# Down and up of a step side by side, one tile transposed by VectorE, base splits a pair earlier, no GpSimd drain

## The chip, the cores and the metric

One NeuronCore of one Trainium2 chip runs the kernel. The metric is the device time of one execution in microseconds (us); of the kernel before, three runs gave 684.30 (median), 684.29 and 685.31. A core has the engines TensorE (PE; its weight loads are listed as PEld), VectorE (DVE), ScalarE (ACT), GpSimd (POOL) and SyncE (SP), each with its own instruction stream, which meet only through semaphores.

## The reference, cut to what matters

Two layers, each an adapter chosen per sequence, then a feed-forward part, with a residual. The routed low-rank part of layer 0 is a sum over 8 experts, two of which carry weight.

```python
# x (32 sequences, 64 tokens, 1024), ids (32,)
c  = einsum('bsi,boi->bso', x, L0_cond_weight[ids])          # 16 adapters of 1024x1024
w  = normalised top-2 of softmax(c @ W_router.T)             # 8 experts
h  = einsum('td,erd->ter', c, lora_A)                        # rank 16
x1 = x + c @ W_base.T + b_base + 2 * einsum('ter,eor,te->to', h, lora_B, w)
y  = einsum('bct,bcd->bdt', x1, L1_cond_weights[ids])        # 64x64 mix over a sequence's tokens
t  = y[:, perm].reshape(-1, 16, 64)                          # 16 heads
u  = gelu(einsum('bhd,hdm->bhm', t, up))                     # hidden 256
t  = einsum('bhm,hmd->bhd', u, down)
out = x1 + t[:, argsort(perm)]
```

## The kernel before, in words

The work has two phases. In the adapter phase 16 pairs of sequences, sorted by adapter, go through the 1024x1024 adapter product in fp32 (`adapter_blocks`, 8 blocks of rows for each pair); VectorE turns the result of a pair with 32x32-block transposes (`turn_pair`, L797), TensorE computes router and low-rank products from it (`router`, L437), VectorE makes the routing weights (`route`), TensorE turns them (`turn_hw`) and GpSimd keeps the pair in `c_all`. In the last pair (number 15) the adapters' ring of buffers comes free block by block, and `base_t`, which lies in the same memory, is filled: ScalarE writes the leading part of W_base as fp32r (`base_leading(j)`, L641) and VectorE the rest (`base_rest(j)`, L868). The last pair's own result goes another way: ScalarE and VectorE copy it out (`out_of_acc`), TensorE turns it (`turn`), both copy it again.

The second phase has 4 groups of 8 sequences (512 tokens) and, in each, 8 steps of 128 output rows, 32 steps in all, written as a loop over groups with the steps of a group unrolled (`over_steps`). A step (g, j) of TensorE's queue holds work of three steps: the base product of step j in 4 parts (`base`: for each of two row blocks two fp32r matmuls with `c_hi`, L505, then one each with `c_lo`, L510) and 3 low-rank matmuls (`lora`, L518 to L520), after which VectorE adds bias and residual (`layer0_out`, L916) into one of 4 `xres` buffers; of step j-1 the 4 transposes of that tile to token rows (`to_tokens`, L403), which ScalarE copies to `x1_tok` (`x1_tokens`, L681), the mix (`mix_tokens`, L533), the split of its result into `y_hi` (ScalarE, L690) and `y_lo` (VectorE, L926) and the up product (`up_heads`, L546, 64-row tiles, two heads side by side); of step j-2 the four gelus (ScalarE, L677), the down product (`down_heads`, L555, 64-column tiles, two heads side by side) and the final add (`result`, L932), after which GpSimd stores the tile by an indirect DMA (`store`, L376), and, when that has landed, fetches the next tile into the same buffer (`refill`, L322). In the last step of a group, `c_leading` (ScalarE) and `c_rest` (VectorE, L904) split the next group's `c`.

The order of every engine's queue is written by hand. TensorE's before, in one step:

```python
base(g, j, 0)
to_tokens(j1)
base(g, j, 1)
down_heads(g2, j2)
mix_tokens(g1, j1)
base(g, j, 2)
base(g, j, 3)
lora(g, j)
up_heads(g1, j1)
```

SyncE loads `up_raw` for the next step once `up_rest` has read it, and `down_sb` (two buffers) once a down product is done, in one queue in that order. The eight PSUM banks are all in use: 0 to 3 for up, 4 for `c_ps`, 5 for `tr_ps`, 6 for the mix, 7 for down.

## Time and profile before

| what | value |
|---|---|
| profiled execution | 684.34 us, of it 682.5 us from the first to the last instruction |
| matmuls, weight loads | 3266, 3267 |
| VectorE busy | 277.4 us (41%) |
| ScalarE busy | 158.8 us (23%) |
| GpSimd busy | 128.2 us (19%) |
| DMA | 102.86 MB, mean 151 GB/s |

A timeline row gives start, duration, engine, line, operation, destination and source tiles, and how many instructions are merged in it; in brackets stands how long the engine was idle before it and what ended that. Starts of successive rows on TensorE are the better measure of cost, since matmuls overlap: one may be listed with 0.39 us while the next starts 0.23 us later.

### The profile page before, as it was taken

To read this page: it belongs to the slowest core of one execution; us is meant where nothing else is said; L and a number is where in the kernel's file an instruction comes from. 1 tells how busy PE (TensorE), PEld (TensorE's weight loads), DVE (VectorE), ACT (ScalarE), POOL (GpSimd) and SP (SyncE) were. 2 spreads that over 40 slices of the span, in tenths; PEclk is the share of its full clock that TensorE was granted. 3 is DMA by queue.
4 is the path that set the end of the run, shared out by engine and by line. 5 is a ranking of instruction groups with operands and counts; after the bars stand their busy time and mean duration, and the time that the engine had idled before them with its cause. 6 is when DMAs were issued, how large, how long until landed. Compare 5 with 4: busy or idle time off the path is not lost.

```text
span 682.5 us, 10584 instructions
## 1 busy us (share of the span) xinstructions
PE 641.7 (94%) x3266; PEld 366.1 (54%) x3267; DVE 277.4 (41%) x714; ACT 158.8 (23%) x294; POOL 128.2 (19%) x194
## 2 busy tenths in 40 slices
PE   3899999999999999887999999999999999999992
PEld 3334434434333433374767676767676666666660
DVE  2046666666656666773212421214221225121220
ACT  3100000000000000344232633234333244323241
POOL 5000001111111100300222222222222222222201
PEclk9799999999999999979999999999999999999997
DMA  8998671459595959300222222222222222222200
GB/s 292 411 405 311 241 286 36 172 184 392 191 396 182 402 174 404 106 17 9 77 67 80 63 78 61 79 65 79 61 77 63 79 65 77 62 77 63 78 31 31
DMA packets 42298, 102.86 MB, mean 151 GB/s; under 512 B 8322, under 2 KB 17538, under 8 KB 42242
## 3 DMA queue, kind: packets, MB, share of 16 engines
q1 hardware_dynamic: 34370, 80.24, 32.8%
q0 software_dynamic: 6784, 21.51, 9.4%
q10 hardware_dynamic: 1088, 0.56, 0.3%
q14 instruction: 44, 0.36, 0.2%
q8 instruction: 12, 0.20, 0.1%
HBM read 93.89 MB, written 8.39 MB: 150 GB/s over the span
## 4 chain that ended last, share of the span: by engine, by line
PE 86%; DMA 5%; DVE 2%; issue 2%; SPq 1%; ACT 1%; POOL 0%; ACTq 0%; DVEq 0%; POOLq 0%
PE wide L423 27%; PE bank L505 18%; PE bank L555 9%; PE bank L510 8%; PE wide L546 7%; DMA ring<-adapters_dram 5%; PE bank L533 5%; PE bank L437 4%; PE bank L403 3%; DVE base_t L868 1%; PE bank L518 1%; PE bank L519 1%; PE bank L520 1%; SPq L227 1%; PE bank L443 1%
## 5 line engine op out<-in xcount | busy, mean ns | idle before, releaser
L423 PE MATMUL wide<-ring,x_in 128*64 128x512 f32 x1024 | 228.3, 599 | 7.9 <-DMA ring<-adapters_dram 7.6
L423 PEld LDWEIGHTS wide<-ring,x_in 128*64 128x64 f32 x1024 | 72.8, 137 | 148.0 <-issue 142.5
L505 PE MATMUL bank<-c_hi,base_t 128*128 128x512 f32 x496 | 142.8, 409 | 0.8 <-DVE base_t L868 0.8
L797 DVE STREAM_TRANSPOSE c_pair<-wide 32x256 f32<-32x256 f32 x240 | 107.1, 446 | 63.7 <-issue 34.3
L505 PEld LDWEIGHTS bank<-c_hi,base_t 128*128 128x128 f32 x496 | 86.3, 189 | 25.0 <-issue 11.7
L677 ACT ACTIVATE act_sb<-wide 128x512 f32<-128x512 f32 x128 | 66.3, 603 | 101.7 <-PE wide L546 101.7
L932 DVE TENSOR_TENSOR xres<-bank,xres 128x512 f32<-128x512 f32 x32 | 22.1, 691 | 162.7 <-PE bank L555 162.7
L510 PE MATMUL bank<-c_lo,base_t 128*128 (+1 forms) x248 | 77.0, 391 | 0.0
L376 POOL DMA_INDIRECT out_dram<-xres,row_out x32 | 34.4, 1075 | 208.3 <-DVE xres L932 208.3
L555 PE MATMUL bank<-act_sb,down_sb 128*64 128x512 f32 x256 | 62.0, 605 | 1.5 <-issue 1.5
L637 ACT ACTIVATE small<-small 128x1 f32<-128x1 f32 x16 | 3.2, 203 | 249.1 <-DVE small L833 249.1
L354 POOL COPY c_all<-c_pair 128x512 f32 x30 | 17.5, 610 | 230.0 <-DVE c_pair L797 230.0
L510 PEld LDWEIGHTS bank<-c_lo,base_t 128*128 128x128 f32 x248 | 46.6, 188 | 10.8
L322 POOL DMA_INDIRECT xres<-xT_dram,row_in x32 | 36.1, 1130 | 77.8 <-DMA out_dram<-xres,row_out 74.5
L916 DVE SCALAR_TENSOR_TENSOR xres<-bank,bias,xres 128x512 f32<-128x512 f32 x31 | 23.3, 750 | 59.3 <-PE bank L520 59.3
L533 PEld LDWEIGHTS bank<-mix_sb,x_tok 128*128 128x128 f32 x256 | 31.0, 191 | 25.5 <-issue 24.3
L690 ACT CAST y_hi<-bank 128x512 fp32r<-128x512 f32 x32 | 18.8, 587 | 100.5 <-PE bank L533 100.5
L533 PE MATMUL bank<-mix_sb,x_tok 128*128 (+1 forms) x256 | 37.0, 287 | 0.9 <-ACT x_tok L681 0.9
L437 PE MATMUL bank<-ar_sb,c_pair 128*128 128x136 f32 x256 | 34.1, 289 | 0.8 <-DVE c_pair L806 0.8
L437 PEld LDWEIGHTS bank<-ar_sb,c_pair 128*128 128x128 f32 x256 | 33.2, 202 | 2.0 <-DVE c_pair L806 1.2
L555 PEld LDWEIGHTS bank<-act_sb,down_sb 128*64 128x64 f32 x256 | 15.7, 136 | 31.0 <-issue 30.9
L926 DVE TENSOR_TENSOR y_lo<-bank,y_hi 128x512 fp32r<-128x512 f32 x32 | 22.1, 692 | 21.5 <-ACT y_hi L690 21.1
(111 smaller groups left out, 477.0 us busy)
## 6 DMA issues: line engine op xcount, KB each, us to landing
ring<-adapters_dram SPq DMA_DIRECT2D x120, 512.0 KB, 7.1
x_in<-x_seq_dram SPq DMA_DIRECT2D x32, 256.0 KB, 7.6
up_raw<-up_dram SPq DMA_DIRECT2D x64, 64.0 KB, 2.3
down_sb<-down_dram SPq DMA_DIRECT2D x32, 128.0 KB, 2.3
ar_sb<-lora_a_router_dram ACTq DMA_DIRECT2D x1, 544.0 KB, 4.4
mix_sb<-mix_dram SPq DMA_DIRECT2D x32, 16.0 KB
xres<-xT_dram,row_in POOLq DMA_INDIRECT x32, 3.4
out_dram<-xres,row_out POOLq DMA_INDIRECT x32, 3.1
```

Of the source, the lines that this page charges most:

```text
L322: pool.indirect_dma_start(dst, None, table, bass.IndirectOffsetOnAxis(ap=rows, axis=0)) \
L376: pool.indirect_dma_start(out_rows, bass.IndirectOffsetOnAxis(ap=row_out[:, j:j + 1], axis=0), xres[:, j % XBUF, :], None).then_inc(stored ...
L423: last = pe.matmul(acc[half][h][z * TOK:(z + 1) * TOK, :], x_in[:, half, z, k, :], ring[:, k, z, h * HALF:(h + 1) * HALF], start=(k == 0), ...
L437: last = pe.matmul(router_ps[:, 0:AR], c_pair[:, k, :], ar_sb[:, k, :], start=(k == 0), stop=(k == KT - 1))
L505: pe.matmul(c_bank(g, j)[:, :], base_t[:, j, w, k, :], c_hi[:, k, :], start=(k == 0 and w == 0), stop=False)
L510: last = pe.matmul(c_bank(g, j)[:, :], base_t[:, j, 0, k, :], c_lo[:, k, bass.ds(g * GT, GT)], start=False, stop=False)
L533: last = pe.matmul(y_ps[:, p * P:(p + 1) * P], x1_tok[:, p * P:(p + 1) * P], mix_sb[:, bass.ds(g % 2, 1), p, :].rearrange("c a d -> c (a d)"),
L546: last = pe.matmul(u_ps[2 * m + head][:, :], w[rows, m * P:(m + 1) * P], y[rows, :], start=(n == 0), stop=(n == 2))
L555: last = pe.matmul(d_ps[head * HD:(head + 1) * HD, :], down_sb[:, j % 2, head, m, :], act_sb[:, 2 * m + head, :], start=(m == 0), stop=(m ...
L677: nc.scalar.activation(act_sb[:, i, :], u_ps[i][:, :], ACT.Gelu).then_inc(act_ok, 1)
L797: last = nc.vector.transpose(c_pair[r * SQ:(r + 1) * SQ, :, q * SQ:(q + 1) * SQ], wide[half][q * SQ:(q + 1) * SQ, :, :] .rearrange("p h (k ...
L916: nc.vector.scalar_tensor_tensor(out=xres[:, b, :], in0=c_bank(g, j)[:, :], scalar=bias[:, j:j + 1], in1=xres[:, b, :], op0=ALU.add, op1=A ...
```

## The change

TensorE's queue: in a step, down of step j-2 and up of step j-1 now stand together at the end, after `lora`; the mix of step j-1 stands between base parts 2 and 3; `to_tokens` is gone from all steps but 1 and the last. In its place VectorE transposes the tile by 16 block transposes from `xres` straight to `x1_tok` (`x1_turned`), so the ScalarE copy is gone there too. `down_heads` waits for each half of its gelus apart, and for the result two steps earlier. VectorE's `result` moves from step j-2 to step j-3 of its queue; `gelu` moves from j-2 to j-1 in ScalarE's, and `up_leading` is made a step earlier, behind the gelus. In the last pair, ScalarE begins the base splits before the tanh of pair 14, and VectorE makes three of them (0, 1, 4) before that pair's routing, two behind it, one (5) after the last pair's tiles, and two in step 1. `b_lo` is made before the last pair's tile is turned back; in step 1 base part 3 stands ahead of `to_tokens`, and up no longer waits for that step's tile. The block is closed without GpSimd's drain.

```diff
@@ -54,6 +54,7 @@
 BIG = -3.0e38
 SEQ_BITS = 5
 CS = KT // 2
+SPLIT_ORDER = (0, 1, 4, 2, 3, 5, 6, 7)
 GATHERS = range(PAIRS // 4, PAIRS // 4 + KT)
 
 
@@ -155,7 +156,8 @@
         base_ps = [banks[4:6], banks[2:4]]
         b_ps = banks[0:2]
         sorted_ps = banks[7]
-        u_ps, c_ps, tr_ps, y_ps, d_ps = banks[0:4], banks[4], banks[5], banks[6], banks[7]
+        u_ps, c_ps, y_ps, d_ps = banks[0:4], banks[4], banks[6], banks[7]
+        second_ps, tr_ps = banks[5], (banks[7], banks[5])
 
 
         ids_in, sort_ids_in, perm_in, ar_in, b_in, bias_in, mix_in, up_in = (
...
@@ -207,13 +209,13 @@
         def c_bank(g, j):
 
 
-            return u_ps[3] if early(g, j, 2) and j == 1 else c_ps
+            return second_ps if early(g, j, 2) and j == 1 else c_ps
 
         def early(g, j, n):
 
             return isinstance(g, int) and g * STEPS + j < n
 
-        block = ctx.enter_context(nc.Block())
+        block = ctx.enter_context(nc.Block(no_gpsimd_drain=True))
 
 
         @block.sync
...
@@ -548,9 +550,10 @@
                     last.then_inc(u_done, 1)
 
             def down_heads(g, j):
-                pe.wait_ge(act_ok, (g * STEPS + j) * 4 + 4)
                 pe.wait_ge(down_in[j % 2], (g * (STEPS // 2) + j // 2 + 1) * 16)
+                pe.wait_ge(fin_ok, g * STEPS + j)
                 for m in range(2):
+                    pe.wait_ge(act_ok, (g * STEPS + j) * 4 + 2 * m + 2)
                     for head in range(2):
                         last = pe.matmul(d_ps[head * HD:(head + 1) * HD, :], down_sb[:, j % 2, head, m, :],
                                          act_sb[:, 2 * m + head, :], start=(m == 0), stop=(m == 1),
@@ -559,22 +562,23 @@
 
             def first_step():
 
+                pe.wait_ge(base_ok, 1)
                 for part in range(CS):
                     base(0, 0, part)
-                base(0, 1, 0)
-                base(0, 1, 1)
+                pe.wait_ge(base_ok, 2)
+                for part in range(2):
+                    base(0, 1, part)
                 turn_hw(PAIRS - 1)
                 base(0, 1, 2)
                 pe.wait_ge(b_ok, 1)
                 lora(0, 0)
 
             def second_step():
+                base(0, 1, 3)
                 pe.wait_ge(x1_ok, 1)
-                to_tokens(0)
-                base(0, 1, 3)
+                to_tokens(0, 0)
                 lora(0, 1)
                 mix_tokens(0, 0)
-                pe.wait_ge(x1_ok, 2)
                 up_heads(0, 0)
                 pe.wait_ge(base_ok, KT)
 
@@ -587,24 +591,20 @@
                     return
                 g1, j1 = (g, j - 1) if j >= 1 else (g - 1, STEPS - 1)
                 g2, j2 = (g, j - 2) if j >= 2 else (g - 1, STEPS + j - 2)
-                base(g, j, 0)
-                to_tokens(j1)
-                base(g, j, 1)
+                for part in range(CS - 1):
+                    base(g, j, part)
+                mix_tokens(g1, j1)
+                base(g, j, CS - 1)
+                lora(g, j)
                 down_heads(g2, j2)
-                mix_tokens(g1, j1)
-                base(g, j, 2)
-                base(g, j, 3)
-                lora(g, j)
                 up_heads(g1, j1)
 
-            pe.wait_ge(base_ok, 6)
             over_steps(pe, step)
             pe.wait_ge(x1_ok, LAST)
-            to_tokens(STEPS - 1)
+            to_tokens(STEPS - 1, 1)
             mix_tokens(GROUPS - 1, STEPS - 1)
             down_heads(GROUPS - 1, STEPS - 2)
             up_heads(GROUPS - 1, STEPS - 1)
-            pe.wait_ge(fin_ok, LAST - 1)
             down_heads(GROUPS - 1, STEPS - 1)
 
 
@@ -646,16 +646,19 @@
                     last = nc.scalar.copy(base_rows[:, j, h * KT // 2:(h + 1) * KT // 2, :],
                                           base_ps[j % 2][h][:, :].rearrange("p (k o) -> p k o", o=P))
                 last.then_inc(base_turned, 1)
-            with act.Fori(0, PAIRS - 1) as t:
+            with act.Fori(0, PAIRS - 2) as t:
                 tanh(t)
-            for j in range(0, 6):
+            for j in range(0, 5):
                 base_leading(j)
+            tanh(PAIRS - 2)
             act.wait_ge(b_tr, 1)
-            act.wait_ge(base_ok, 5)
+            act.wait_ge(base_ok, 3)
             for h in range(2):
                 last = nc.scalar.copy(b_hi[:, h * KT // 2:(h + 1) * KT // 2, :],
                                       b_ps[h][:, :].rearrange("p (j o) -> p j o", o=P))
             last.then_inc(b_hi_ok, 1)
+            for j in range(5, 7):
+                base_leading(j)
             seqs = last_seqs(act)
             out_of_acc(PAIRS - 1, 1)
             turned(PAIRS - 1)
...
@@ -691,44 +694,37 @@
 
             def step(g, j):
                 g1, j1 = (g, j - 1) if j >= 1 else (g - 1, STEPS - 1)
-                g2, j2 = (g, j - 2) if j >= 2 else (g - 1, STEPS + j - 2)
                 if early(g, j, 1):
-                    act.wait_ge(base_ok, 6)
+                    act.wait_ge(base_ok, 5)
                     act.wait_ge(c_kept, PAIRS * 2)
                     act.wait_ge(last_kept, 4)
                     for part in range(CS):
                         c_leading(g, part)
+                    base_leading(7)
+                    up_leading(g, j)
                     tanh(PAIRS - 1)
+                    act.wait_ge(base_ok, 6)
                     act.wait_ge(hw_t_ok, PAIRS * 2)
                     hw_leading(g)
-                    base_leading(6)
-                    base_leading(7)
-                elif j == 0:
+                    return
+                if j == 0:
                     act.wait_ge(c_done, g * STEPS)
                     hw_leading(g)
                 splits = j == STEPS - 1 and not (isinstance(g, int) and g == GROUPS - 1)
-                if not early(g, j, 2):
-                    for i in range(4):
-                        gelu(g2, j2, i)
+                if early(g, j, 2):
+                    x1_tokens(0)
                 if splits:
-                    c_leading(g + 1, 0)
-                if not early(g, j, 1):
-                    x1_tokens(g1, j1)
+                    for part in range(CS - 1):
+                        c_leading(g + 1, part)
+                y_leading(g1, j1)
                 if splits:
-                    c_leading(g + 1, 1)
-                if not early(g, j, 1):
-                    up_leading(g1, j1)
-                    y_leading(g1, j1)
-                if splits:
-                    c_leading(g + 1, 2)
-                    c_leading(g + 1, 3)
+                    c_leading(g + 1, CS - 1)
+                for i in range(4):
+                    gelu(g1, j1, i)
+                up_leading(g, j)
 
             over_steps(act, step)
-            for i in range(3):
-                gelu(GROUPS - 1, STEPS - 2, i)
-            x1_tokens(GROUPS - 1, STEPS - 1)
-            gelu(GROUPS - 1, STEPS - 2, 3)
-            up_leading(GROUPS - 1, STEPS - 1)
+            x1_tokens(1)
             y_leading(GROUPS - 1, STEPS - 1)
             for i in range(4):
                 gelu(GROUPS - 1, STEPS - 1, i)
@@ -880,21 +876,24 @@
                 pair(i * 2 + 2, 0)
             pair(PAIRS - 3, 1)
             turn_pair(PAIRS - 2, 0)
+            for j in SPLIT_ORDER[0:3]:
+                base_rest(j)
             hw_turned(PAIRS - 3)
             route(PAIRS - 2)
-            for j in range(0, 6):
+            for j in SPLIT_ORDER[3:5]:
                 base_rest(j)
             seqs = last_seqs(dve)
             out_of_acc(PAIRS - 1, 1)
-            turned(PAIRS - 1)
-            keep_last(1, seqs)
-            hw_turned(PAIRS - 2)
             dve.wait_ge(b_hi_ok, 1)
             for h in range(2):
                 ks = slice(h * KT // 2, (h + 1) * KT // 2)
                 last = nc.vector.tensor_tensor(b_lo[:, ks, :], b_ps[h][:, :].rearrange("p (j o) -> p j o", o=P),
                                                b_hi[:, ks, :].bitcast(F32), ALU.subtract)
             last.then_inc(b_ok, 1)
+            turned(PAIRS - 1)
+            keep_last(1, seqs)
+            hw_turned(PAIRS - 2)
+            base_rest(SPLIT_ORDER[5])
             dve.wait_ge(bias_in, KT * 16)
 
 
@@ -931,35 +930,51 @@
                 dve.wait_ge(d_done, g * STEPS + j + 1)
                 nc.vector.tensor_tensor(xres[:, b, :], d_ps[:, :], xres[:, b, :], ALU.add).then_inc(fin_ok, 1)
 
+            def x1_turned(g, j):
+
+                b = j % XBUF
+                dve.wait_ge(x1_ok, g * STEPS + j + 1)
+                for q in range(P // SQ):
+                    for f in range(P // SQ):
+                        last = nc.vector.transpose(
+                            x1_tok[q * SQ:(q + 1) * SQ, :].rearrange("p (c f) -> p c f", f=P)[:, :, f * SQ:(f + 1) * SQ],
+                            xres[f * SQ:(f + 1) * SQ, b, :].rearrange("p (c q t) -> p c q t", c=GP, t=SQ)[:, :, q, :])
+                last.then_inc(x1_tok_ok, 1)
+
             def step(g, j):
                 g1, j1 = (g, j - 1) if j >= 1 else (g - 1, STEPS - 1)
-                g2, j2 = (g, j - 2) if j >= 2 else (g - 1, STEPS + j - 2)
+                g3, j3 = (g, j - 3) if j >= 3 else (g - 1, STEPS + j - 3)
                 if early(g, j, 1):
                     for part in range(CS):
                         c_rest(g, part)
                     route(PAIRS - 1)
                     hw_turned(PAIRS - 1)
+                    hw_rest(g)
+                    layer0_out(g, j)
+                    return
+                if not early(g, j, 3):
+                    result(g3, j3)
+                up_rest(g1, j1)
+                if early(g, j, 2):
+                    for i in SPLIT_ORDER[6:8]:
+                        base_rest(i)
                 if j == 0:
                     hw_rest(g)
                 splits = j == STEPS - 1 and not (isinstance(g, int) and g == GROUPS - 1)
                 if splits:
                     c_rest(g + 1, 0)
                     c_rest(g + 1, 1)
-                if not early(g, j, 2):
-                    result(g2, j2)
-                if not early(g, j, 1):
-                    up_rest(g1, j1)
-                    y_rest(g1, j1)
+                y_rest(g1, j1)
                 if splits:
                     c_rest(g + 1, 2)
                 layer0_out(g, j)
+                if not (isinstance(g, int) and g == GROUPS - 1 and j == STEPS - 1):
+                    x1_turned(g, j)
                 if splits:
                     c_rest(g + 1, 3)
-                if early(g, j, 2) and j == 1:
-                    base_rest(6)
-                    base_rest(7)
-
-            over_steps(dve, step)
+
+            over_steps(dve, step, 3)
+            result(GROUPS - 1, STEPS - 3)
             up_rest(GROUPS - 1, STEPS - 1)
             y_rest(GROUPS - 1, STEPS - 1)
             result(GROUPS - 1, STEPS - 2)
```

## Rows read from the trace of the kernel before

**Rows 1.** The page: busy time, share and count of TensorE; granted clock in 40 slices.
```profile
PE 641.7 (94%) x3266; PEld 366.1 (54%) x3267; DVE 277.4 (41%) x714; ACT 158.8 (23%) x294; POOL 128.2 (19%) x194
...
PEclk9799999999999999979999999999999999999997
```
**Rows 2.** Timeline of TensorE over one step of the second phase.
```profile
341.93 1.19 PE L505 MATMUL bank<-c_hi,base_t 128*128 128x512 f32 x4
342.96 0.62 PE L510 MATMUL bank<-c_lo,base_t 128*128 x2
343.42 0.60 PE L403 MATMUL bank<-ident,xres 128*128 128x128 f32 x4
343.77 1.18 PE L505 MATMUL bank<-c_hi,base_t 128*128 128x512 f32 x4
344.79 0.62 PE L510 MATMUL bank<-c_lo,base_t 128*128 x2
345.34 1.94 PE L555 MATMUL bank<-act_sb,down_sb 128*64 128x512 f32 x8
347.21 1.16 PE L533 MATMUL bank<-mix_sb,x_tok 128*128 x8
...
349.59 1.07 PE L505 MATMUL bank<-c_hi,base_t 128*128 128x512 f32 x4
350.50 0.62 PE L510 MATMUL bank<-c_lo,base_t 128*128 x2
...
351.41 0.39 PE L520 MATMUL bank<-hw_lo,b_hi 128*128 x1
351.73 0.50 PE L546 MATMUL wide<-y_hi,up_hi 64*128 64x512 f32 x2
...
353.31 1.20 PE L505 MATMUL bank<-c_hi,base_t 128*128 128x512 f32 x4
```
**Rows 3.** Timeline of TensorE: the first matmuls of step 2 and of step 31.
```profile
319.13 1.18 PE L505 MATMUL bank<-c_hi,base_t 128*128 128x512 f32 x4 [0.81 <-DVE base_t L868]
...
649.46 1.20 PE L505 MATMUL bank<-c_hi,base_t 128*128 128x512 f32 x4
```
**Rows 4.** Timeline of VectorE: the add behind that step's lora.
```profile
351.94 0.75 DVE L916 SCALAR_TENSOR_TENSOR xres<-bank,bias,xres 128x512 f32<-128x512 f32 x1 [2.22 <-PE bank L520]
```
**Rows 5.** Timeline of VectorE: the transposes of one pair in the adapter phase.
```profile
204.65 7.34 DVE L797 STREAM_TRANSPOSE c_pair<-wide 32x256 f32<-32x256 f32 x16 [1.90 <-PE wide L423]
```
**Rows 6.** Groups by shape, 340 to 680 us: busy, mean ns, idle before.
```profile
L932 DVE TENSOR_TENSOR xres<-bank,xres 128x512 f32<-128x512 f32 x30 | 20.7, 691 | 151.0 <-PE bank L555 151.0
...
L921 DVE TENSOR_TENSOR up_lo<-up_raw,up_hi 128x256 fp32r<-128x256 f32 x29 | 12.1, 416 | 3.0 <-ACT up_hi L686 3.0
```
**Rows 7.** The page's DMA issues: count, KB, median us from issue to landing.
```profile
up_raw<-up_dram SPq DMA_DIRECT2D x64, 64.0 KB, 2.3
```
**Rows 8.** Timeline of GpSimd: one fetch alone, one beside VectorE's `c_rest`.
```profile
352.74 1.06 POOL L322 DMA_INDIRECT xres<-xT_dram,row_in  x1 [2.52 <-DMA out_dram<-xres,row_out]
...
387.46 1.73 POOL L322 DMA_INDIRECT xres<-xT_dram,row_in  x1 [2.55 <-DMA out_dram<-xres,row_out]
```
**Rows 9.** Timeline of TensorE from the last pair to step 1.
```profile
292.32 1.97 PE L403 MATMUL bank<-ident,c_tok 128*128 128x128 f32 x8 [4.88 <-ACT c_tok L620]
295.08 3.76 PE L437 MATMUL bank<-ar_sb,c_pair 128*128 128x136 f32 x16 [0.78 <-DVE c_pair L806]
...
310.98 0.66 PE L403 MATMUL bank<-ident,xres 128*128 128x128 f32 x4 [0.84 <-DVE xres L916]
...
316.67 0.50 PE L546 MATMUL wide<-y_hi,up_hi 64*128 64x512 f32 x2 [2.06 <-DVE xres L916]
```
**Rows 10.** Timeline of VectorE in the last pair: the base splits.
```profile
284.48 6.89 DVE L868 TENSOR_TENSOR base_t<-base_rows,base_t 128x1024 fp32r<-128x1024 f32 x6
```
**Rows 11.** Timeline of TensorE behind the last step.
```profile
668.50 1.94 PE L555 MATMUL bank<-act_sb,down_sb 128*64 128x512 f32 x8 [1.51 <-issue]
```
**Rows 12.** Instructions of line 64, the block's end: count, min/median/max ns, starts.
```profile
L64 POOLq DRAIN  x1: 7268/7268/7268, 675.0 to 675.0; - x1
```

More of the change, by code:

```diff
@@ L189, in build, with over_steps @@
         bias_rows = b_base.rearrange("(d a) -> d a", a=1)
-        def over_steps(eng, step):
-            step(0, 0)
-            step(0, 1)
+        def over_steps(eng, step, first=2):
+            for j in range(first):
+                step(0, j)
             with eng.Fori(0, GROUPS - 1) as g:
-                for j in range(2, STEPS + 2):
+                for j in range(first, STEPS + first):
                     step(g + j // STEPS, j % STEPS)
-            for j in range(2, STEPS):
+            for j in range(first, STEPS):
                 step(GROUPS - 1, j)
@@ L521, in lora, with to_tokens @@
                           start=False, stop=True).then_inc(c_done, 1)
-            def to_tokens(j):
-                transposes([tr_ps], [xres[:, j % XBUF, p * P:(p + 1) * P] for p in range(GP)], tr_done)
+            def to_tokens(j, way):
+                transposes([tr_ps[way]], [xres[:, j % XBUF, p * P:(p + 1) * P] for p in range(GP)], tr_done)
             def mix_tokens(g, j):
@@ L677, in gelu, with x1_tokens @@
                 nc.scalar.activation(act_sb[:, i, :], u_ps[i][:, :], ACT.Gelu).then_inc(act_ok, 1)
-            def x1_tokens(g, j):
-                act.wait_ge(tr_done, g * STEPS + j + 1)
-                nc.scalar.copy(x1_tok[:, :], tr_ps[:, :]).then_inc(x1_tok_ok, 1)
+            def x1_tokens(way):
+                act.wait_ge(tr_done, way + 1)
+                nc.scalar.copy(x1_tok[:, :], tr_ps[way][:, :]).then_inc(x1_tok_ok, 1)
             def up_leading(g, j):
```

## The prediction

> **What bounds the kernel now.** I read the page's busy shares first: TensorE is busy 94% of the span, VectorE, the next, 41% [rows 1]. A busy TensorE need not be a well used one, so the timeline of one step comes next, read by the starts of successive rows [rows 2]. There is no idle bracket in it: weight loads, transposes and matmuls follow each other. From the start of step 2 to that of step 31 the distance is 649.46 - 319.13 = 330.33 us for 29 steps, 11.39 us each [rows 3]. In this phase an instruction taken off TensorE's queue is time gained, as long as what replaces it elsewhere arrives before TensorE asks for it. At the phase's beginning and end it is otherwise: there TensorE waits for VectorE and ScalarE, and at the very end for GpSimd.
>
> **The sum** is made against the profiled execution, 684.34 us, which is the median of the runs (684.30) within 0.04. I go through it in four places.
>
> **1. The steps.** The four transposes take 343.77 - 343.42 = 0.35 us. The base part behind them takes 344.79 - 343.77 = 1.02 for its four L505, where one behind other base work takes 350.50 - 349.59 = 0.91: each change of kind costs the follower 0.11. Both go: 0.46. Up begins 351.73 - 351.41 = 0.32 after the last lora matmul, against 0.91/4 = 0.23 inside a row of such matmuls: 0.09 for going from full tiles to row tiles. Before, a step enters down from base (344.79 to 345.34 is 0.55, the two L510 need 342.96 to 343.42 = 0.46, so 0.09) and up from lora (0.09); now down is entered from lora and up from down, whose 1.87 us (345.34 to 347.21) hold the way out of column tiles already. So one entry of 0.09 goes. The mix, now behind base, may lose a little of its entry too; unseen in these rows, it is between 0 and 0.06, and I take 0.02, nearer the end at which nothing happens, because no row shows the mix behind full tiles in a steady step [rows 2]. A step becomes 11.39 - 0.57 = 10.82; 29 steps give 16.5 us (bounds 0.45 and 0.62 a step: 13.0 and 18.0).
>
> The page TensorEngine Tiling (Array Packing) of the Trainium skill, section Key Properties, says that changing the tiling mode drains TensorE. By that rule alone one drain of four goes; the rows above price it at 0.09, a small part of the gain.
>
> **Does the replacement arrive in time?** Count from the start of down, D, which now follows lora. VectorE's add starts 351.94 - 351.73 = 0.2 after TensorE's next group and takes 0.75 [rows 2, 4], so transposes start at D + 1.0. No such transpose is in the trace; the nearest is 32x256, 16 of them in 7.34 us or 459 ns each [rows 5]. From 256 to 512 elements a VectorE instruction grows from 416 to 691 ns, 1.07 ns an element [rows 6], so 128 elements fewer are 137 ns less: 322 ns, 5.2 us for 16. The source is SBUF and not PSUM, which I count as no difference; the upper bound is the untouched 7.34, the lower 4.5. The tile is ready at D + 6.25. TensorE asks for it after down (1.87), up (353.31 - 351.73 = 1.58) and three base parts (1.03 + 0.46, then 0.91 + 0.46 twice: 4.23), at D + 7.68 [rows 2]. Slack 1.4 us: hidden. At the upper bound the tile comes at D + 8.4, 0.7 late.
>
> The page VectorE: DVE Perf Modes of the Trainium skill, section Rules for kernel authors, speaks against this edit: transpose 128x128 on TensorE if PSUM will do as destination. The rows agree that TensorE is far quicker at it (0.35 us and a copy against about 5.2); what they add is which engine the 0.35 us is taken from.
>
> What else moves, in each queue. VectorE: behind the transposes stand `result` (0.69) and `up_rest` (0.42) [rows 6], done at about D + 7.4; then y's rest, which needs the mix, and the next add, at D + 11. Its step holds 2.55 + 5.2 = 7.8 us of 10.8. In a group's last step four `c_rest` (as long as a base split of the same size, 1.15, below) and `hw_rest` are added; walking them in order, the third delays the add by about 0.6, the transposes end about 1.2 us before the mix, and the fourth `c_rest` is done some 2 us before base part 3 wants it. So I cost the three borders at nothing; without that cover each would be 1 to 2 us. ScalarE, busy 23% in all [rows 1], loses the copy; its gelus run right behind up, and the down that wants them comes 7 us later. The added wait of down for `result` two steps back is met 4 us early; behind it in TensorE's queue stand down and up. `result` comes some 8 us later than before, so the store and refetch by GpSimd start later, about 9 us in all, against 21 us until the buffer is wanted. SyncE: the load of `up_raw` stands in its queue behind the wait for a down that is now at the step's end; it is issued behind down (D + 1.9) and `down_sb`'s load, and lands 2.3 us after issue [rows 7], about D + 5.5. ScalarE wants it behind its gelus, at about D + 5, and VectorE's `up_rest` at D + 7: half a microsecond on ScalarE, hidden by the transposes. All cost nothing.
>
> Beside VectorE's SBUF work GpSimd's fetch instruction is stretched from 1.06 to 1.73 us [rows 8]; there is slack of 7 us for it.
>
> **2. The beginning.** Before, TensorE waits 4.88 us for the last pair's tile: VectorE makes six splits of 6.89/6 = 1.15 us from 284.48 on [rows 9, 10] and only then copies the tile. Now three come before the routing, mostly in VectorE's idle time (delaying the routing by about 0.5), and two remain behind it: 285.0 + 2.3 + 0.7 gives the tile at 288.0 where `turn` started at 292.32: 4.2 us. The granted clock has a digit 7 in the 18th slice, 290 to 307 [rows 1], where these waits lie, and the 16 router passes of 3.76 us [rows 9] are at the 1.2 GHz level; with a wait of 1 us instead of 4.88 I take them at 2.4 GHz, half as long. Not all of that 1.9 + 0.9 counts, because then base waits about 0.5 for the first `c_lo`, which VectorE now delivers behind `b_lo` and one split: 2.1 us. In steps 0 and 1 the wait of `to_tokens` for the add (0.84) is filled by base part 3; the wait before up goes from 2.06 to about 1.6; the wait for the last splits, 0.81, goes [rows 3, 9]. Sum 4.2 + 2.1 + 0.8 + 0.5 + 0.8 = 8.4 us (bounds 4.2, the first term alone, and 9.5).
>
> **3. The end.** Step 31 saves its transposes, 0.46, and the 0.09. ScalarE now has one gelu and `up_leading` before the token copy (about 1.0), for which the mix waits. The last down, which waits 1.51 for all four gelus, starts after two [rows 11]: 0.9 earlier. Sum 0.5 us gained (bounds: 1.0 lost, 1.4 gained).
>
> **4. The drain.** GpSimd's DRAIN of 7268 ns starts at 675.0, when the last store has landed, and the span ends at 682.5 [rows 12]. Nothing else happens meanwhile. Without it: 7.2 us gained. Bounds 0, if the same work is then waited for elsewhere or outside the span, and 7.3.
>
> **Forecast:** 16.5 + 8.4 + 0.5 + 7.2 = 32.6; 684.3 - 32.6 = **651.7 us**. Bounds: 13.0 + 4.2 - 1.0 + 0 = 16.2 (668.1) and 18.0 + 9.5 + 1.4 + 7.3 = 36.2 (648.1).
>
> **The rivals.**
> *The beginning gives only its first term.* The clock stays low behind the shorter wait, or base waits for `c_lo`. For it: VectorE has the same work, only shifted. 651.7 + 4.2 = 655.9.
> *The drain does not vanish.* Its time is real bookkeeping for GpSimd's DMAs, and the end may wait for it in another way. 651.7 + 7.2 = 658.9. Against it: DMA had landed and no engine worked on.
> *The transposes cost per instruction, not per element.* Then 7.34 us, 0.7 late in 29 steps: 20.6 less gain, 672.3. For it: half-sized instructions never run here. Against: 416 against 691 ns.
> *Slower: VectorE and GpSimd stretch each other.* If the 16 transposes are stretched as GpSimd's fetch is (1.73/1.06 = 1.63), they take 8.5 us, the mix waits 1.9 us in every step, 54 us in all: 706. It decides from 7.75 us for 16 on (484 ns each), where the wait of 1.1 us a step eats all 32.6. Against it: only GpSimd's side of such an overlap is seen stretched, and its own work takes a quarter of a step.
>
> **How the numbers follow.** Forecast 0.67, beginning 0.11, drain 0.10, per-instruction cost 0.07, slower 0.03, nothing gained overall 0.02. The first alone spans 648.5 to 654.5; the range that leaves out the last three kinds is 648.0 to 660.0. All cases but the last two are faster by over 0.2% (1.4 us), about what a measurement of this kernel can tell from no change: faster 0.95, same 0.01, slower 0.04.
>
> **What would show it.** Right: starts of `base` part 0 10.8 us apart in TensorE's timeline, no idle bracket before the mix; a group of 16 x 30 transposes 32x128 of about 320 ns; idle before `turn` about 1 us and router passes at full granted clock; no POOL DRAIN in the block's end, and a span ending 0.3 us after the last store lands. Wrong: an idle time of TensorE before L533 put down to VectorE, step 2 starting later than 313, transposes above 410 ns, a DRAIN or a longer time outside the span.

## The result and the profile after

The changed kernel takes 651.83 us (median; 650.76 to 653.02), the kernel before, measured beside it, 684.46. The ratio is 0.952, 95% interval 0.950 to 0.954. The forecast was 651.7 us. The profiled execution took 651.0 us with a span of 649.1, against 684.34 and 682.5: the span is 33.4 us shorter.

The total agrees better than its terms. Cut at the same five events, the two traces give:

| stretch | before, us | after, us | gained | forecast |
|---|---|---|---|---|
| start to `turn_hw` behind the last adapter block | 287.1 | 286.1 | 1.0 | 0 |
| from there to the start of step 2 | 32.0 | 24.8 | 7.3 | 8.4 |
| 29 steps | 330.3 | 311.2 | 19.1 | 16.5 |
| start of step 31 to the end of the last `result` | 21.7 | 23.0 | -1.3 | 0.5 |
| last `result` to the end | 11.3 | 4.0 | 7.3 | 7.2 |

The first row is scatter: the same kernel, profiled again, reached this event at 287.85, later than before. In that second trace the stretch up to step 2 took 25.5 us and the one behind the start of step 31 took 21.3, so these two rows would read 6.5 and 0.4 gained; the 29 steps and the last row are the same within 0.1.

The page of the changed kernel, busy shares and granted clock (compare rows 1): TensorE has 120 matmuls fewer and a higher share, VectorE goes from 41% to 65%, and the low clock of the 18th slice is gone in this execution.

```profile
PE 621.0 (96%) x3146; PEld 356.4 (55%) x3147; DVE 423.4 (65%) x1194; ACT 141.6 (22%) x262; POOL 130.7 (20%) x194
...
PEclk9799999999999999999999999999999999999998
```

The chain that ended last goes over TensorE by 76% of the span. Its timeline over one step (answers to rows 2):

```profile
332.43 1.20 PE L507 MATMUL bank<-c_hi,base_t 128*128 128x512 f32 x4
...
336.20 0.62 PE L512 MATMUL bank<-c_lo,base_t 128*128 x2
336.66 1.05 PE L535 MATMUL bank<-mix_sb,x_tok 128*128 x8
337.47 1.17 PE L507 MATMUL bank<-c_hi,base_t 128*128 128x512 f32 x4
...
339.38 0.39 PE L522 MATMUL bank<-hw_lo,b_hi 128*128 x1
339.69 1.94 PE L558 MATMUL bank<-act_sb,down_sb 128*64 128x512 f32 x8
341.56 0.51 PE L548 MATMUL wide<-y_hi,up_hi 64*128 64x512 f32 x2
...
343.16 1.20 PE L507 MATMUL bank<-c_hi,base_t 128*128 128x512 f32 x4
```

The step is 343.16 - 332.43 = 10.73 us. The mix holds TensorE for 337.47 - 336.66 = 0.81 us, where before, behind down, it held it for 0.91 (from 347.21, rows 2, to the base part behind it). Down still takes 1.87, and up follows it with no entry of its own. No row has an idle bracket. The base part behind the mix, before:

```profile
348.12 1.17 PE L505 MATMUL bank<-c_hi,base_t 128*128 128x512 f32 x4
```

VectorE in the same stretch, and the group of its new transposes (answers to rows 5 and 6):

```profile
329.96 5.05 DVE L939 STREAM_TRANSPOSE x_tok<-xres 32x128 f32<-32x128 f32 x16
335.05 0.69 DVE L931 TENSOR_TENSOR xres<-bank,xres 128x512 f32<-128x512 f32 x1
...
L939 DVE STREAM_TRANSPOSE x_tok<-xres 32x128 f32<-32x128 f32 x480 | 145.3, 303 | 7.2
```

16 transposes take 5.05 us, 316 ns each; the estimate was 322. They end at 335.01 and the mix starts at 336.66.

TensorE at the beginning (answers to rows 9), the start of step 2 being 310.87 (rows 3: 319.13), and the start of step 31 at 622.06:

```profile
286.11 0.33 PE L445 MATMUL bank<-ident,hw 128*128 128x128 f32 x1
287.92 1.10 PE L405 MATMUL bank<-ident,c_tok 128*128 128x128 f32 x8 [1.48 <-DVE c_tok L785]
289.80 2.12 PE L439 MATMUL bank<-ar_sb,c_pair 128*128 128x136 f32 x16 [0.79 <-DVE c_pair L802]
...
293.42 0.74 PE L512 MATMUL bank<-c_lo,base_t 128*128 128x512 f32 x2 [0.55 <-DVE c_lo L903]
...
303.21 0.47 PE L520 MATMUL bank<-hw_hi,b_hi 128*128 128x512 f32 x1 [0.74 <-DVE hw_lo L908]
...
309.29 0.50 PE L548 MATMUL wide<-y_hi,up_hi 64*128 64x512 f32 x2 [1.49 <-DVE y_lo L925]
...
310.87 1.20 PE L507 MATMUL bank<-c_hi,base_t 128*128 128x512 f32 x4
```

And behind the last step (answers to rows 11), the last `result` at 644.38 and GpSimd's last store:

```profile
622.06 1.20 PE L507 MATMUL bank<-c_hi,base_t 128*128 128x512 f32 x4
...
635.55 1.76 PE L535 MATMUL bank<-mix_sb,x_tok 128*128 128x128 f32 x8 [2.11 <-ACT x_tok L684]
637.24 2.95 PE L558 MATMUL bank<-act_sb,down_sb 128*64 128x512 f32 x8
...
642.37 1.97 PE L558 MATMUL bank<-act_sb,down_sb 128*64 128x512 f32 x8 [0.58 <-ACT act_sb L680]
...
644.38 0.69 DVE L931 TENSOR_TENSOR xres<-bank,xres 128x512 f32<-128x512 f32 x1 [3.44 <-PE bank L558]
...
645.89 1.05 POOL L378 DMA_INDIRECT out_dram<-xres,row_out  x1 [2.82 <-DVE xres L931]
```

The wait before the last mix is 2.11 us, and the down behind it takes 2.95 instead of 1.94.

### The profile page after: what moved, and what is told of

Read it like the earlier page. It is cut to its first block, busy times and chain, and to the rows that moved or that the text cites. A ratio compares the mean times of both kernels' runs of the same rounds, so it can differ in the third digit from the quotient of the medians.

```text
span 649.1 us, 10832 instructions
## 1 busy us (share of the span) xinstructions
PE 621.0 (96%) x3146; PEld 356.4 (55%) x3147; DVE 423.4 (65%) x1194; ACT 141.6 (22%) x262; POOL 130.7 (20%) x194
## 4 chain that ended last, share of the span: by engine, by line
PE 76%; issue 7%; SPq 6%; DMA 5%; DVE 4%; ACT 0%; DVEq 0%; POOL 0%; POOLq 0%; ACTq 0%
PE wide L425 21%; PE bank L507 18%; PE bank L558 9%; PE bank L512 8%; PE wide L548 8%; DMA ring<-adapters_dram 5%; PE bank L535 5%; PE bank L439 3%; SPq L229 3%; SPq L242 2%; PE bank L520 1%; PE bank L521 1%; PE bank L522 1%; DVE c_pair L793 1%; DVE c_lo L903 1%
## 5 line engine op out<-in xcount | busy, mean ns | idle before, releaser
L939 DVE STREAM_TRANSPOSE x_tok<-xres 32x128 f32<-32x128 f32 x480 | 145.3, 303 | 7.2
L507 PEld LDWEIGHTS bank<-c_hi,base_t 128*128 128x128 f32 x512 | 91.5, 188 | 26.9 <-issue 10.8
L512 PE MATMUL bank<-c_lo,base_t 128*128 (+1 forms) x256 | 79.2, 390 | 0.5 <-DVE c_lo L903 0.5
L378 POOL DMA_INDIRECT out_dram<-xres,row_out x32 | 35.8, 1119 | 199.2 <-DVE xres L931 199.2
L356 POOL COPY c_all<-c_pair 128x512 f32 x30 | 19.3, 670 | 229.1 <-DVE c_pair L793 229.1
L324 POOL DMA_INDIRECT xres<-xT_dram,row_in x32 | 33.9, 1059 | 67.8 <-DMA out_dram<-xres,row_out 64.6
L535 PEld LDWEIGHTS bank<-mix_sb,x_tok 128*128 128x128 f32 x256 | 33.7, 193 | 5.3 <-ACT x_tok L684 2.8
L535 PE MATMUL bank<-mix_sb,x_tok 128*128 (+1 forms) x256 | 34.6, 279 | 2.1 <-ACT x_tok L684 2.1
L693 ACT CAST y_hi<-bank 128x512 fp32r<-128x512 f32 x32 | 18.8, 586 | 77.2 <-PE bank L535 74.2
L439 PE MATMUL bank<-ar_sb,c_pair 128*128 128x136 f32 x256 | 32.5, 280 | 0.8 <-DVE c_pair L802 0.8
L439 PEld LDWEIGHTS bank<-ar_sb,c_pair 128*128 128x128 f32 x256 | 31.6, 193 | 1.8 <-DVE c_pair L802 1.0
```

What stands on the lines that cost most here:

```text
L324: pool.indirect_dma_start(dst, None, table, bass.IndirectOffsetOnAxis(ap=rows, axis=0)) \
L378: pool.indirect_dma_start(out_rows, bass.IndirectOffsetOnAxis(ap=row_out[:, j:j + 1], axis=0), xres[:, j % XBUF, :], None).then_inc(stored ...
L439: last = pe.matmul(router_ps[:, 0:AR], c_pair[:, k, :], ar_sb[:, k, :], start=(k == 0), stop=(k == KT - 1))
L507: pe.matmul(c_bank(g, j)[:, :], base_t[:, j, w, k, :], c_hi[:, k, :], start=(k == 0 and w == 0), stop=False)
L512: last = pe.matmul(c_bank(g, j)[:, :], base_t[:, j, 0, k, :], c_lo[:, k, bass.ds(g * GT, GT)], start=False, stop=False)
L535: last = pe.matmul(y_ps[:, p * P:(p + 1) * P], x1_tok[:, p * P:(p + 1) * P], mix_sb[:, bass.ds(g % 2, 1), p, :].rearrange("c a d -> c (a d)"),
```

## The experiments

The first is the changed kernel again, beside which the next three ran.

> The changed kernel once more, as the measure for the kernels that run beside it. 650.7 to 653.0 us. Steps 10.73 us apart, step 2 about 8 us earlier than before, the tail behind step 31 about 1.3 us longer.

651.93 us, ratio 0.952 (0.949 to 0.954); steps 10.73. The other two numbers missed: step 2 starts at 313.37, 5.8 us earlier than before and not 8, and the tail is 0.4 us shorter than before and not 1.3 longer. Apart from the scatter of the adapter phase, the trace differs from the first in two places, and they turn out to matter: the router passes behind a wait of 1.48 us took 3.62 us (first trace 2.12), and down behind the wait before the last mix took 1.94 (first trace 2.95).

```profile
291.54 3.62 PE L439 MATMUL bank<-ar_sb,c_pair 128*128 128x136 f32 x16 [0.78 <-DVE c_pair L802]
...
637.94 1.16 PE L535 MATMUL bank<-mix_sb,x_tok 128*128 128x128 f32 x8 [2.00 <-ACT x_tok L684]
639.03 1.94 PE L558 MATMUL bank<-act_sb,down_sb 128*64 128x512 f32 x8
```

**The drain alone**, on the kernel before:

```diff
-        block = ctx.enter_context(nc.Block())
+        block = ctx.enter_context(nc.Block(no_gpsimd_drain=True))
```

> The kernel before with only the block's GpSimd drain left out. If the drain is pure waiting at the end: 7.2 to 7.3 us less than before (677.1 us), no POOL DRAIN, the same 1.8 us outside the span. If its work is waited for elsewhere: the same 684 us, either as another long instruction at the end or as more time outside the span.

678.33 us against 685.11 of before on the same chip, 6.8 less, ratio 0.989 (0.986 to 0.993). The last `result` ends at 672.3 and the span at 676.4: 4.1 us, where it was 11.3: 7.2 less. The time outside the span is 678.16 - 676.4 = 1.8, as before. The drain was pure waiting; it does not come back elsewhere.

**The transposes back on TensorE**, the new order kept (ScalarE's copy, which comes back with them, is not shown):

```diff
-                for part in range(CS - 1):
-                    base(g, j, part)
+                base(g, j, 0)
+                to_tokens(j1, 1)
+                base(g, j, 1)
+                base(g, j, 2)
                 mix_tokens(g1, j1)
...
-                if not (isinstance(g, int) and g == GROUPS - 1 and j == STEPS - 1):
-                    x1_turned(g, j)
```

> The changed kernel with the tile transposed by TensorE again (behind base part 0) and copied by ScalarE; down and up stay side by side. If the transposes cost TensorE 0.35 and the base part behind them 0.11: a step of 11.19 us, 13.3 us more, about 665. If the gain of a step came from the new order alone: under 655. In the tail the copy waits as in the changed kernel, so no difference there.

665.83 us (ratio 0.972, 0.969 to 0.974), 13.9 more than the changed kernel. Its steps are 11.19 us (from the add of step 2 to that of step 31, 320.15 to 644.76, over 29). By the same adds the kernel before has steps of 11.387, this one 11.193 and the changed kernel 10.726. So the transposes are worth 0.47 a step, and the new order 0.19. In the trace the four transposes take 0.35 and the base part behind them 1.02:

```profile
403.36 0.60 PE L405 MATMUL bank<-ident,xres 128*128 128x128 f32 x4
403.71 1.17 PE L507 MATMUL bank<-c_hi,base_t 128*128 128x512 f32 x4
404.73 0.63 PE L512 MATMUL bank<-c_lo,base_t 128*128 x2
```

**Down back in the middle of the base parts:**

```diff
-                for part in range(CS - 1):
-                    base(g, j, part)
+                base(g, j, 0)
+                base(g, j, 1)
+                down_heads(g2, j2)
+                base(g, j, 2)
                 mix_tokens(g1, j1)
                 base(g, j, CS - 1)
                 lora(g, j)
-                down_heads(g2, j2)
                 up_heads(g1, j1)
```

> The changed kernel with down moved back between base parts 1 and 2 of the step, so that it no longer stands beside up; the mix stays between parts 2 and 3, VectorE still transposes. If each change between kinds of tile costs its entry (0.09) and the first matmuls behind it (0.11): a step of 10.73 + 0.20 = 10.93 us, 29 steps 5.8 us more, about 657.5. If standing side by side is worth only the one entry: 10.82 and 654.4. If it is worth nothing and the gain is all from the transposes: 10.73 and 651.8.

746.34 us, ratio 1.089 (1.085 to 1.094): all three expectations missed, by 89 to 95 us. I had priced the kinds of tile and had forgotten the wait that moves with down. Down writes the one PSUM bank in which the down of the step before left its product; `result` has to read that out first, and VectorE makes that `result` only behind its 16 transposes:

```profile
407.94 5.05 DVE L940 STREAM_TRANSPOSE x_tok<-xres 32x128 f32<-32x128 f32 x16
413.03 0.69 DVE L932 TENSOR_TENSOR xres<-bank,xres 128x512 f32<-128x512 f32 x1
...
413.97 3.57 PE L558 MATMUL bank<-act_sb,down_sb 128*64 128x512 f32 x8 [2.41 <-DVE xres L932]
...
442.11 1.94 PE L558 MATMUL bank<-act_sb,down_sb 128*64 128x512 f32 x8 [2.20 <-DVE xres L932]
```

TensorE waits 2.2 to 2.4 us in each step, and 3.9 at borders of groups. A plain step becomes 13.3 us; in seven of them down takes some 3.5 us in place of 1.94, at a granted clock near 0.5, and the step some 14.9. So the two edits are not independent: with VectorE's transposes in its queue, down must stand late in the step. The run says nothing on the price of the tile kinds; the next one was made for that.

**Down late, but apart from up:**

```diff
-                for part in range(CS - 1):
+                for part in range(CS):
                     base(g, j, part)
                 mix_tokens(g1, j1)
-                base(g, j, CS - 1)
+                down_heads(g2, j2)
                 lora(g, j)
-                down_heads(g2, j2)
                 up_heads(g1, j1)
```

> The changed kernel with a step's queue on TensorE as base 0 to 3, mix, down, lora, up: down is apart from up by the lora matmuls, but late enough that VectorE's result of two steps back is there (in the kernel with down between base parts 1 and 2 it was not, and TensorE waited there in every step). If entering up from lora costs what the trace before showed (0.09) and nothing else moves: steps of 10.82 us, 2.6 us more in all, 654.5. If only the order of waits matters and not what stands beside what: 10.73. The mix is wanted 5.8 + 1.4 = 7.2 us behind lora and ready at 6.1, so no wait there.

660.07 us, ratio 0.963 (0.961 to 0.965), 8.1 more than the changed kernel where at most 2.6 were expected. Against its second trace, 7.8 of them are in the 29 steps and 1.9 between the adds of steps 0 and 2; the tail is 1.5 shorter. Steps inside a group are 10.92 us, 0.19 more than in the changed kernel; the borders of groups add a wait for `c_lo` (0.46 us at one of them) and bring the mean to 11.00. The expected 0.09 was half of it:

```profile
406.87 1.05 PE L535 MATMUL bank<-mix_sb,x_tok 128*128 x8
407.86 1.94 PE L558 MATMUL bank<-act_sb,down_sb 128*64 128x512 f32 x8
409.72 0.50 PE L520 MATMUL bank<-hw_hi,b_hi 128*128 128x512 f32 x1
410.06 0.39 PE L521 MATMUL bank<-hw_hi,b_lo 128*128 128x512 f32 x1
...
410.61 0.50 PE L548 MATMUL wide<-y_hi,up_hi 64*128 64x512 f32 x2
```

The mix before down holds TensorE for 0.99 instead of 0.81 (+0.18), the first lora matmul behind down for 0.34 instead of 0.23 (+0.11), up is entered at the old 0.09, and from the changed order 0.10 behind the mix and 0.09 of lora to down are saved. 0.18 + 0.11 + 0.09 - 0.19 = 0.19. Why down costs 0.18 to enter from the mix, and 0.09 from base or lora, no run shows.

**How much slack the transposes have:** 4 and 8 more of them in each step, ahead of the 16 (one run each).

```diff
+                for n in range(4):   # 8 in the other
+                    q, f = n % 4, n // 4
+                    nc.vector.transpose(spare[...], xres[...])
                 for q in range(P // SQ):
                     for f in range(P // SQ):
                         last = nc.vector.transpose(
```

> The changed kernel with 4 more block transposes in each step, into a spare tile, ahead of the 16 (their result is used by nothing). 20 instead of 16 take 1.26 us longer (315 ns each). By the slack counted in the trace (tile ready at D + 6.1, wanted at D + 7.6, D the start of down) about 0.2 us of slack is left: no wait before the mix, steps stay at 10.73 us, within 0.05. If VectorE were already the bound, each step would be 1.26 us longer, 36 us in all.

658.53 us, 6.6 more: right inside a group and missed at its borders. Steps inside a group stay at 10.73 us; but each of the three borders between groups now costs 1.6 us more (two distances between adds are 12.08 and 11.04 where they were 11.17 and 10.39), with a wait before the mix that the changed kernel does not have, and step 2 costs 1.3. Together 6.1 of the 6.6 us.

```profile
383.29 1.16 PE L536 MATMUL bank<-mix_sb,x_tok 128*128 x8 [0.75 <-DVE x_tok L945]
```

> The same with 8 more, 2.5 us longer: the slack of about 1.5 us is used up and TensorE waits about 1.0 us before the mix in every step: steps of 11.7 us, about 29 us more in all, 680. If the slack is larger than the trace lets one count (3 us, say), no change. If VectorE is the bound already: 73 us more.

689.87 us, 38 more and slower than the kernel before on the same chip (684.69). Steps inside a group are 11.7 to 11.8 us, about 1.0 longer, as expected; borders lose some 2 us beyond that. VectorE is 72% busy, and yet TensorE waits for it before the mix of nearly every step, 25.9 us in 28 waits:

```profile
403.11 1.15 PE L536 MATMUL bank<-mix_sb,x_tok 128*128 x8 [1.03 <-DVE x_tok L945]
```

**The base splits behind the routing again:**

```diff
-            with act.Fori(0, PAIRS - 2) as t:
+            with act.Fori(0, PAIRS - 1) as t:
                 tanh(t)
             for j in range(0, 5):
                 base_leading(j)
-            tanh(PAIRS - 2)
...
-            for j in SPLIT_ORDER[0:3]:
-                base_rest(j)
             hw_turned(PAIRS - 3)
             route(PAIRS - 2)
-            for j in SPLIT_ORDER[3:5]:
+            for j in SPLIT_ORDER[0:5]:
                 base_rest(j)
```

> The changed kernel with the five base splits all behind the routing of pair 14, and ScalarE's tanh of that pair before its splits, as it was before; the rest of the beginning stays changed. VectorE copies the last tile 3 x 1.15 = 3.5 us later less 0.5 by which the routing is earlier: turn starts 3 us later, behind an idle time of about 4.5 us. If the length of that wait decides the granted clock: transposes of turn and router run at half clock again (router 3.76 instead of 2.12 us), together another 2 us partly hidden, step 2 starts 4 to 5 us later than in the changed kernel. If the low clock has nothing to do with the wait: 3 us later, router passes still 2.1 us.

657.22 us, ratio 0.959 (0.956 to 0.962), 5.3 more than the changed kernel. TensorE waits 5.29 us, `turn` starts 5.6 us behind `turn_hw` (changed: 1.8), the first add comes 23.3 us behind it (changed: 18.1, and 18.8 in the second trace; before: 23.1). So this edit is worth 4.4 to 5.2 us; up to the first add it is the whole gain, since with the splits back nothing is left of it (23.3 against 23.1 before). And the router runs at the low clock:

```profile
292.71 1.97 PE L405 MATMUL bank<-ident,c_tok 128*128 128x128 f32 x8 [5.29 <-ACT c_tok L620]
295.46 3.54 PE L439 MATMUL bank<-ar_sb,c_pair 128*128 128x136 f32 x16 [0.79 <-DVE c_pair L801]
```

**The token copy of the last tile between gelus 1 and 2**, in place of behind all four and the up copy:

```diff
+                last_step = isinstance(g, int) and g == GROUPS - 1 and j == STEPS - 1
                 for i in range(4):
+                    if last_step and i == 2:
+                        x1_tokens(1)
                     gelu(g1, j1, i)
                 up_leading(g, j)
...
-            x1_tokens(1)
             y_leading(GROUPS - 1, STEPS - 1)
```

> The changed kernel with ScalarE's copy of the last tile moved between gelus 1 and 2 of the step before, instead of behind all four and the up copy. The mix of the last step can start 1.6 us earlier, TensorE waits 0.4 instead of 2.1 us before it. If the wait also costs the clock: mix and down run at full clock (0.9 + 1.9 instead of 1.7 + 2.9) and up starts about 3.2 us earlier, the whole 3 us shorter, about 649. If the clock there has another cause: 1.6 us shorter or less, as down then waits for its gelus.

650.01 us, ratio 0.949 (0.946 to 0.952). From the last add to the end of the last result it takes 12.6 us; the changed kernel took 15.6 and 13.9 in its two traces, the kernel before 11.8 without the 1.9 us of the down that has been moved there. TensorE waits 0.68 us before the mix, and all behind it ran at full clock. By the medians it is 1.9 us faster than the changed kernel; the intervals of the two ratios overlap, so its traces carry this more than its times.

```profile
635.26 1.16 PE L535 MATMUL bank<-mix_sb,x_tok 128*128 128x128 f32 x8 [0.68 <-ACT x_tok L684]
636.35 1.94 PE L558 MATMUL bank<-act_sb,down_sb 128*64 128x512 f32 x8
```

**The wait before the last mix filled**, order as in the changed kernel (one run):

```diff
             to_tokens(STEPS - 1, 1)
+            for n in range(22):
+                pe.transpose(y_ps[:, 0:P], ident[:, :], ident[:, :])
```

> The changed kernel with 22 transposes of the identity behind the last tile's (into the mix's bank, nothing reads them), which fill TensorE's wait of 2.1 us before the last mix. If the wait is what lets the clock fall there: mix and down behind it at full clock (0.9 + 1.9 us), 13.9 us from the last add to the last result as in the profile of the changed kernel that ran full there. If the clock falls for another reason it may still be low there: 15.6 us.

650.38 us; 14.1 us from the last add to the last result, down at 1.94. It fits that the wait lets the clock fall, but a single run shows no more. Of the six traces that have this wait unfilled, at 2.0 to 2.1 us, four ran low behind it (the changed kernel's first, transposes back on TensorE, 4 more transposes, base splits late) and two at full clock; the three in which it is filled or cut to 0.68 all ran at full clock.

**Base part 0 of step 2 ahead of up in step 1**, on top of the moved token copy:

```diff
                 lora(0, 1)
                 mix_tokens(0, 0)
+                pe.wait_ge(base_ok, 4)
+                base(0, 2, 0)
                 up_heads(0, 0)
...
-                for part in range(CS - 1):
+                for part in range(1 if early(g, j, 3) else 0, CS - 1):
                     base(g, j, part)
```

> The kernel with the token copy of the last tile between gelus 1 and 2, and in addition base part 0 of step 2 ahead of up in step 1, where TensorE waits 1.49 us for VectorE's y. The wait is filled by work of 1.37 us that is taken from step 2: 1.3 us less than with the copy alone, about 648.7. If y_lo is late for another reason than the wait seen (VectorE's order), the wait moves to the mix of step 2, since its tile comes no earlier: there it is wanted 4.2 us behind up and VectorE needs 0.75 + 5.05 behind y_lo; then half or nothing is gained (649.4 to 650).

649.86 us, ratio 0.949 (0.948 to 0.951): the same as without it. The wait of 1.49 us before up is filled, and most of it appears again before the mix of step 2, put down to VectorE's transposes, which were not earlier:

```profile
316.91 1.16 PE L535 MATMUL bank<-mix_sb,x_tok 128*128 128x128 f32 x8 [1.05 <-DVE x_tok L943]
```

## Why the prediction was right, point by point

**The steps: mechanism right, one term too small.** Forecast 0.57 a step with 0.62 as the upper bound, measured 0.66. The transposes with the base part behind them were put at 0.46 and are 0.47. The order of the queue was put at 0.11 and is 0.19: the term that was mis-sized is the mix, "between 0 and 0.06, and I take 0.02". It held TensorE for 0.91 behind down and holds it for 0.81 behind base. The trace of before had the rule in it: a part of base behind another kind of work takes 0.11 longer, and the mix behind down was such a follower. I applied this to base alone. That the 0.10 is the follower's cost is read from rows; no run isolates it. The drain at a change of tiling mode (the Trainium skill, TensorEngine Tiling (Array Packing), Key Properties) is there in the rows as an entry of 0.09 us from full tiles; from column tiles (down) to row tiles (up), which is such a change too, the rows show none. The order was worth twice 0.09, because the mix as a follower counted too. The 0.19 of the order comes from the kernel with the transposes back on TensorE. The 0.19 that taking down from up costs is made of other terms (0.18 + 0.11 + 0.09 - 0.19), so the equal size confirms nothing.

**The transposes in time: right**, and shown on both sides. 16 are ready 1.6 us before the mix starts in a plain step, against a slack of 1.4 in the working; 20 still fit there; with 24 TensorE waits, 0.9 us in the mean of 28 waits. The rival that prices them by the instruction (459 ns each) falls with 316. The walk through a group's last step holds too: the transposes end 1.3 us before the mix, and 1.2 was the working. What the working had too generously is the point at which the change turns slower than before. It said 7.75 us for the 16, from plain steps alone; at some 7.6 us (24 transposes) the kernel was already slower by 5 us in one run, because the borders of groups have less slack: 20 already wait there.

**The contention rival falls.** GpSimd's fetch takes a mean of 1059 ns in the changed kernel against 1130 before, and VectorE's transposes never more than 5.05 us for 16. They do overlap: from 329 us on each fetch of the changed kernel runs beside transposes for 0.5 us or more, and takes 1.05 or 1.06 us as it does alone. They do not stretch each other.

```profile
619.02 1.06 POOL L324 DMA_INDIRECT xres<-xT_dram,row_in  x1 [2.31 <-DMA out_dram<-xres,row_out]
...
619.48 5.05 DVE L939 STREAM_TRANSPOSE x_tok<-xres 32x128 f32<-32x128 f32 x16
```

The stretched fetch of rows 8 ran beside `c_rest` and then `hw_rest` (1.73 to 1.79 us in the three such places of the kernel before); the rival carried its factor over to another kind of instruction.

**The beginning: 7.3 us instead of 8.4.** `turn` starts 1.8 us behind `turn_hw` instead of 5.2: 3.4 gained where the working had 4.2. The term that was too small is the delay of the routing by the three splits, "about 0.5": VectorE starts that routing at 281.34 instead of 281.04, in a trace that is 1.0 us ahead at that point, so 1.3 late, and ends it 1.4 late.

```profile
281.04 0.30 DVE L824 COPY h_l<-bank 128x136 f32<-128x136 f32 x1 [1.38 <-PE bank L437]
...
281.34 0.29 DVE L820 COPY h_l<-bank 128x136 f32<-128x136 f32 x1
```

(The first row is of the kernel before, the second of the changed one.) From there to the first add it gained 1.6 against 2.1, and that only in this trace: "I take them at 2.4 GHz" did not hold in the second, where the first add comes 0.8 later. Of the ten traces with this short wait it held in four. From the first add to step 2 it gained 8.96 - 6.68 = 2.3 against 2.1; this part is read from the two traces alone, no run undoes its edits.

**The tail: wrong sign.** Forecast 0.5 us gained and at worst 1.0 lost, measured 1.3 lost. The two terms of the sum were a token copy 1.0 later and a down 0.9 earlier. The first was in place (wait 2.11 instead of 0.87), the second is visible (wait 0.58 instead of 1.51). Missing was the clock: mix and down behind the wait took 1.69 + 2.89 us between starts where the second trace shows 1.09 + 1.87, together 1.6 us. The working put the clock here at nothing and gave no reason. In the second trace, at full clock, the stretch gained 0.4, close to the forecast: the two terms were right and the clock is what turned the sign. The moved copy shows that most of the wait was not needed.

**The drain: right**, 7.3 us less from the last `result` to the end in the changed kernel and 7.2 with the drain alone left out.

So the total of 651.7 against 651.83 owes something to luck: 2.6 us too little in the steps against 1.1 and 1.8 too much at the two ends, and 1.0 us of scatter in the adapter phase of the profiled execution. The steps and the tail both lie outside the bounds that the working gave them.

## What to carry to other kernels

Where a bounding engine's queue has no gaps, price an edit by the distance of starts of the rows around it, and count the follower of every change of kind, whatever that follower is. When an instruction is moved in such a queue, list the waits that move with it and ask where the engine that answers them stands in its own queue by then: down in another place cost 94 us with the same work. Slack must be counted at the tightest step of a loop (here the borders of groups), since that one sets how much more the hidden engine can take.

## What the runs showed of the hardware

The granted clock of TensorE behind a wait was not the same from one execution to the next. At the beginning TensorE waits for the last pair's tile, turns it with 8 transposes, waits 0.8 us more and runs the 16 router passes. Three traces have 4.9 to 5.3 us for the first wait: the transposes then take 1.97 us and the passes 3.5 to 4.0, both at the lower level, 1.2 GHz (the kernel before has a granted clock of 0.50 from 292 to 294 and from 295 to 298 us). Ten traces have 1.4 to 1.5 us, with the same instructions: the transposes take 1.1 us in all ten, the passes 2.1 us in four of them and 3.6 to 3.8 in six (granted 0.55 from 291.6 to 295.2 us in the changed kernel's second trace). In the kernel with down in the middle TensorE waits 2.2 to 2.4 us in nearly every step; down then takes 1.94 us in 20 of 27 plain steps and about 3.5 in seven:

```profile
357.44 1.94 PE L558 MATMUL bank<-act_sb,down_sb 128*64 128x512 f32 x8 [2.42 <-DVE xres L932]
...
482.33 3.52 PE L558 MATMUL bank<-act_sb,down_sb 128*64 128x512 f32 x8 [2.33 <-DVE xres L932]
```

What decides between the two stays open; no run here isolates it. In these traces a short wait often cost more than its length: 0.6 to 0.9 us more at the beginning in six of ten, 1.6 to 1.7 in the tail in four of six. A single profile is a poor witness for a term of 1 to 2 us behind one.
